# One GpSimd chain for two layer norms, a reordered start and looped expert programs in a Mamba and MoE block

## What is computed

```python
x = x + mamba(layernorm(x))      # in_proj 256 -> 2*512, causal conv of 4 taps, silu,
                                 # delta = softplus(dt_proj(...) + b), 16 states per channel:
                                 # h[t] = exp(delta*A)*h[t-1] + delta*B*xc ; y = h.C + D*xc
                                 # out_proj(y * silu(z))
x = x + moe(layernorm(x))        # shared: sq_relu(x @ Ws1) @ Ws2
                                 # routed: top 2 of 8 experts, prob = trunc(softmax weight)
```

## Time and profile before

| What | Value |
|---|---|
| Median of 3 runs | 1568.24 us |
| The profiled execution's own time | 1566.09 us |
| Its span, first to last instruction | 1564.0 us |
| Busy share PE / DVE / ACT / POOL | 93% / 94% / 80% / 90% |
| Chain that ended last, by engine | DVE 30%, ACT 19%, PE 18%, issue 16%, POOL 11% |
| DMA over the span | 106.49 MB, mean 68 GB/s |
| Granted TensorE clock | 0.999 |

### The profile page before, as it was taken

How to read it: one execution, slowest core, us unless ns; L and a number is a source line. 1 busy time by engine, 2 the same in 40 slices (tenths; PEclk the granted TensorE clock), 3 DMA queues, 4 the chain that set the end, 5 groups by cost and what they waited for, 6 DMA issues and landing times.

```text
span 1564.0 us, 39669 instructions
## 1 busy us (share of the span) xinstructions
PE 1452.4 (93%) x15308; PEld 1129.9 (72%) x15308; DVE 1474.4 (94%) x1773; ACT 1258.2 (80%) x2100; POOL 1410.5 (90%) x1248
## 2 busy tenths in 40 slices
PE   8789999999999999999999999999999999998987
PEld 4566777776776777777776777777777677777876
DVE  6999999999999999999999999999999999998886
ACT  7987887887888888887887888888887887788762
POOL 2899999999999999999999989999998999999994
PEclk9999999999999999999999999999999999999999
DMA  5103031040402204031040402304031040301301
GB/s 165 56 3 136 2 109 57 9 157 3 145 20 69 96 3 163 2 97 69 7 159 3 137 28 57 109 3 163 2 98 67 3 149 2 137 15 53 113 15 42
DMA packets 78514, 106.49 MB, mean 68 GB/s; under 512 B 42289, under 2 KB 67761, under 8 KB 70130
## 3 DMA queue, kind: packets, MB, share of 16 engines
q1 hardware_dynamic: 78322, 103.92, 20.5%
...
## 4 chain that ended last, share of the span: by engine, by line
DVE 30%; ACT 19%; PE 18%; issue 16%; POOL 11%; DMA 2%; SPq 2%; DVEq 1%; ACTq 0%; POOLq 0%
DVE hs L966 26%; POOL hs L1254 9%; PE BX L236 8%; ACT da L630 8%; PE Y L296 4%; SPq L1383 2%; DMA cb<-c_scratch 2%; PE Y L260 2%; ACT xc L697 1%; ACT xp L665 1%; PE PB L346 1%; ACT x2n L767 1%; ACT u L735 1%; DVE st L978 1%; DVE Y L997 1%
## 5 line engine op out<-in xcount | busy, mean ns | idle before, releaser
L1254 POOL TENSOR_TENSOR hs<-hs,cb 128x1024 f32<-128x1024 f32 x512 | 1211.3, 2367 | 65.6 <-DVE hs L966 43.6
L966 DVE TENSOR_TENSOR_SCAN hs<-da,BX 128x512 f32<-128x512 f32 x1024 | 1165.5, 1201 | 57.9 <-PE BX L236 48.4
L630 ACT ACTIVATE da<-delta,a_neg 128x511 f32<-128x511 f32 (+1 forms) x1024 | 663.5, 711 | 24.9 <-DVE hs L966 24.4
L260 PEld LDWEIGHTS Y<-ident,hs 128*128 128x128 f32 x4096 | 463.7, 141 | 96.5 <-issue 61.5
L260 PE MATMUL Y<-ident,hs 128*128 128x128 f32 x4096 | 511.5, 273 | 11.3 <-POOL hs L1254 11.2
L236 PE MATMUL BX<-bd,uT 32*128 32x128 f32 x8192 | 300.4, 283 | 85.3 <-DVE hs L966 80.3
L236 PEld LDWEIGHTS BX<-bd,uT 32*128 32x128 f32 x8192 | 251.6, 186 | 145.4 <-DVE hs L966 143.0
L296 PE MATMUL Y<-xnT,w_in 128*128 128x512 f32 x240 | 117.6, 612 | 0.9 <-ACT xnT L646 0.9
L665 ACT ACTIVATE xp<-Y 128x512 f32<-128x512 f32 x60 | 35.9, 598 | 99.4 <-PE Y L296 99.0
L321 PE MATMUL PA<-w_in,xnT 128*128 128x512 f32 x240 | 114.4, 599 | 0.0
L997 DVE SCALAR_TENSOR_TENSOR Y<-xp,w_conv,Y 128x512 f32<-128x512 f32 x120 | 88.8, 740 | 2.3 <-ACT Y L667 0.6
...
## 6 DMA issues: line engine op xcount, KB each, us to landing
...
c_scratch<-dbc SPq DMA_DIRECT2D x64, 8.0 KB, 1.5
```

Of the source, the lines that this page charges most:

```text
L260: mm = e.matmul(Y[(G * c + g) % 2][:, t * P:(t + 1) * P], hs[:, k % HR, q, t * P:(t + 1) * P], ident[:, :], is_transpose=True, start=False ...
L630: e.activation(da[:, k % DR, q, h:], delta[:, g, h:], ACT.Exp, scale=a_neg[:, g, n:n + 1]).then_inc(s_da, 1)
L966: e.tensor_tensor_scan(hs[:, k % HR, q, :], da[:, k % DR, q, :], BX[:, :].rearrange("p (t n) -> p n t", n=RT)[:, n % RT, :], float(c % HV) ...
L1254: e.tensor_tensor(hs[:, k % HR, :, :], hs[:, k % HR, :, :], cb[:, Q * p:Q * p + Q, :], ALU.mult).then_inc(s_hc, 1)
```

## The change

It has three parts.

1. In chunks 1 to 12 POOL computes `rstd` and `shift` of both norms in one chain over eight columns instead of two over four, at step 21; the statistics tiles of the two norms lie side by side for that. In chunk 0 the first norm's chain moves from step 25 to step 21. Chunks 13 to 15 keep the second norm's chain at step 21.
2. In the preparation of chunk 0, ACT's norm of chunk 1 stands behind the second silu; `dbc` is evacuated by DVE and the first `u` computed by DVE; the z tiles 1, 2 and 3 and the first skip product are made at other places; the first decay is split around the copy of `uT`. Eight matmuls of the identity into `PA` are added on PE in chunk 0 at step 3.
3. The routed programs of PE, ACT and DVE become loops over the chunks, with DVE shifting `prob` by one chunk in each pass.

The core of the diff, where `BOTH` is (1, 12); left out are the declarations, the counts of the semaphores that the joint chain shifts, the move of ACT's norm of chunk 1 out of its old place, the split of `act_exp`, POOL's wait in place of its first `u`, and the routed program of ScalarE:

```diff
@@ -457,17 +460,17 @@
             e.wait_ge(s_const, 7)
             pe_dbc(e, 0, 0)
             pe_dbc(e, 0, 1)
-            pe_z_first(e, 3, (0,))
             pe_dt(e, 0, 0)
             pe_bt(e, 0)
             pe_dt(e, 0, 1)
-            pe_z_first(e, 3, (1,))
-            pe_z_first(e, 2)
+            pe_z_first(e, 3)
             pe_ut(e, 0, 0)
+            pe_z_first(e, 2, (0,))
             e.wait_ge(s_d1_out, 1)
             pe_bx(e, 0)
             pe_trc(e, 1, 0)
             pe_trc(e, 1, 1)
+            pe_z_first(e, 2, (1,))
             for c in range(NQ):
                 for s in range(S):
                     k = S * c + s
@@ -483,6 +486,11 @@
                         pe_ut(e, c, 2)
                     if c == 0 and s in (0, 4, 8, 12):
                         pe_xp(e, G + s // 4)
+                    if c == 0 and s == 3:
+
+                        e.wait_ge(s_pa_out, a_use["trc", 1, 1] + 1)
+                        for _ in range(8):
+                            e.matmul(PA[:, 0:P], ident[:, :], ident[:, :], start=True, stop=True)
                     if c and on(c + 1) and s in (4, 12):
                         pe_xp(e, G * c + s // NP + 6)
                     if s == 28 and on(c + 1):
@@ -813,12 +820,12 @@
             act_xp_first(e, 2)
             act_xp_first(e, 3)
             act_silu_first(e, 1)
+            act_norm(e, 1)
             act_silu_first(e, 2)
             act_z_first(e, 0)
-            act_z_first(e, 1)
             act_silu_first(e, 3)
             e.preload_act_table_set(EXPS)
-            act_dbc(e, 0)
+            act_z_first(e, 1)
             e.wait_ge(s_wt, 16 * 9)
             e.activation(a_neg[:, :, :], a_log[:, :, :], ACT.Exp).then_inc(s_aneg, 1)
             e.wait_ge(s_aneg, 1)
@@ -826,14 +833,14 @@
             act_softplus(e, 0, 0)
             act_softplus(e, 0, 1)
             e.wait_ge(s_aneg, 2)
-            act_exp(e, 0)
+            act_exp(e, 0, (0,))
             act_ut(e, 0, 0)
+            act_exp(e, 0, (1,))
             act_z_first(e, 3)
-            act_z_first(e, 2)
             act_exp(e, 1)
             act_trc(e, 1, 0)
             act_trc(e, 1, 1)
-            act_skip(e, 0, 0)
+            act_z_first(e, 2)
             act_exp(e, 2)
             for c in range(NQ):
                 for s in range(S):
@@ -1123,10 +1132,18 @@
             dve_stats(e, 2, 0)
             dve_stats(e, 2, 1)
             dve_aggr(e, 2)
+            e.wait_ge(s_pa, a_use["dbc", 0, 0] + 1)
+            e.tensor_copy(dbc[0:FX, :].rearrange("f (j q t) -> f q j t", j=J, q=RT),
+                          PA[0:FX, :].rearrange("f (q j t) -> f q j t", j=J, q=RT)).then_inc(s_pa_out, 1)
             dve_stats(e, 3, 0)
             dve_stats(e, 3, 1)
             dve_bd(e, 0)
             dve_delta(e, 0, 0)
+            e.wait_ge(s_pb_out, b_use["dt", 0, 0] + 1)
+            e.wait_ge(s_xc, 1)
+            e.tensor_tensor(u[:, 0, :].rearrange("p (j q t) -> p q j t", j=J, q=RT),
+                            delta[:, 0, :].rearrange("p (q j t) -> p q j t", j=J, q=RT),
+                            xc[:, 0, :].rearrange("p (q j t) -> p q j t", j=J, q=RT), ALU.mult).then_inc(s_u, 1)
             dve_bd(e, 1)
             dve_delta(e, 0, 1)
             dve_bd(e, 2)
@@ -1276,24 +1293,30 @@
         def pool_rstd(e, c):
             e.wait_ge(s_mv, TB * (c + 1))
             e.wait_ge(s_xn, c)
-            e.tensor_tensor(ve[:, :], mv[:, :, 1], epsv[:, :], ALU.add).then_inc(s_ve, 1)
-            e.tensor_tensor(neg[:, :], mv[:, :, 0], minus[:, :], ALU.mult).then_inc(s_neg, 1)
+            n = TB
+            if BOTH[0] <= c - 3 <= BOTH[1]:
+                n = 2 * TB
+                e.wait_ge(s_mv2, TB * (c - 3))
+                e.wait_ge(s_xn2, c - 4)
+            e.tensor_tensor(ve_b[:, 0:n], mv_b[:, 0:n, 1], epsv[:, 0:n], ALU.add).then_inc(s_ve, 1)
+            e.tensor_tensor(neg_b[:, 0:n], mv_b[:, 0:n, 0], minus[:, 0:n], ALU.mult).then_inc(s_neg, 1)
             e.wait_ge(s_ve, c + 1)
-            e.tensor_tensor(rstd[:, :], ve[:, :], mhalf[:, :], ALU.pow).then_inc(s_rs, 1)
+            e.tensor_tensor(rstd_b[:, 0:n], ve_b[:, 0:n], mhalf[:, 0:n], ALU.pow).then_inc(s_rs, 1)
             e.wait_ge(s_neg, c + 1)
             e.wait_ge(s_rs, c + 1)
-            e.tensor_tensor(shift[:, :], neg[:, :], rstd[:, :], ALU.mult).then_inc(s_sh, 1)
+            e.tensor_tensor(shift_b[:, 0:n], neg_b[:, 0:n], rstd_b[:, 0:n], ALU.mult).then_inc(s_sh, 1)
 
         def pool_rstd2(e, c):
             e.wait_ge(s_mv2, TB * (c + 1))
             e.wait_ge(s_xn2, c)
-            e.tensor_tensor(ve2[:, :], mv2[:, :, 1], epsv[:, :], ALU.add).then_inc(s_ve2, 1)
-            e.tensor_tensor(neg2[:, :], mv2[:, :, 0], minus[:, :], ALU.mult).then_inc(s_neg2, 1)
-            e.wait_ge(s_ve2, c + 1)
-            e.tensor_tensor(rstd2[:, :], ve2[:, :], mhalf[:, :], ALU.pow).then_inc(s_rs2, 1)
-            e.wait_ge(s_neg2, c + 1)
-            e.wait_ge(s_rs2, c + 1)
-            e.tensor_tensor(shift2[:, :], neg2[:, :], rstd2[:, :], ALU.mult).then_inc(s_sh2, 1)
+            n = c + 1 - BOTH[1]
+            e.tensor_tensor(ve2, mv2[:, :, 1], epsv[:, 0:TB], ALU.add).then_inc(s_ve2, 1)
+            e.tensor_tensor(neg2, mv2[:, :, 0], minus[:, 0:TB], ALU.mult).then_inc(s_neg2, 1)
+            e.wait_ge(s_ve2, n)
+            e.tensor_tensor(rstd2, ve2, mhalf[:, 0:TB], ALU.pow).then_inc(s_rs2, 1)
+            e.wait_ge(s_neg2, n)
+            e.wait_ge(s_rs2, n)
+            e.tensor_tensor(shift2, neg2, rstd2, ALU.mult).then_inc(s_sh2, 1)
 
         def pool_gap(e, c):
             e.wait_ge(s_max, TB * (c + 1))
@@ -1334,11 +1357,11 @@
                             pool_u(e, c + 1, 0)
                         if s == 31:
                             pool_u(e, c + 1, 1)
-                    if s == 21 and on(c - 1):
+                    if s == 21 and c > BOTH[1]:
                         pool_rstd2(e, c - 1)
                     if s == 30 and on(c - 1):
                         pool_gap(e, c - 1)
-                    if s == 25 and on(c + 3):
+                    if s == 21 and on(c + 3):
                         pool_rstd(e, c + 3)
 
 
@@ -1485,43 +1509,55 @@
...
         def routed_tensor(e):
             e.wait_ge(r_w, 32)
-            for c in range(NQ):
-                e.wait_ge(r_x, 16 * (c + 1))
+            with e.Fori(0, NQ) as c:
+                e.wait_ge(r_x, 16 * c + 16)
                 for i in range(NE):
-                    m = NE * c + i
-                    e.wait_ge(r_re, m)
+                    if i:
+                        e.wait_ge(r_re, NE * c + i)
                     for kk in range(KD):
                         mm = e.matmul(PA[:, :], wr1[:, i, kk, :], xnT[0][:, kk, :], start=(kk == 0), stop=(kk == KD - 1))
                     mm.then_inc(r_h, 1)
-                    e.wait_ge(r_sq, m + 1)
-                    e.wait_ge(r_add, TB * m)
+                    e.wait_ge(r_sq, NE * c + i + 1)
+                    if i:
+                        e.wait_ge(r_add, TB * NE * c + TB * i)
                     for t in range(TB):
                         mm = e.matmul(Y[t // 2][:, (t % 2) * DM:(t % 2 + 1) * DM], hT[:, t * P:(t + 1) * P], wr2[:, i, :],
                                       start=True, stop=True)
                     mm.then_inc(r_y, 1)
 
...
         def routed_vector(e):
-            for c in range(NQ):
-                e.wait_ge(r_acc, 16 * (c + 1))
+            rest = da[:, :, :, :].rearrange("p k q t -> p (k q t)")[:, 0:(NQ - 1) * TB * NE].rearrange(
+                "p (c t n) -> p c t n", c=NQ - 1, t=TB)
+            with e.Fori(0, NQ) as c:
...
-                    m = NE * c + i
-                    e.wait_ge(r_y, m + 1)
-                    e.wait_ge(r_add, TB * m)
+                    e.wait_ge(r_y, NE * c + i + 1)
+                    if i:
+                        e.wait_ge(r_add, TB * NE * c + TB * i)
                     for t in range(TB):
                         e.scalar_tensor_tensor(
                             out=x1[:, t, :], in0=Y[t // 2][:, (t % 2) * DM:(t % 2 + 1) * DM],
-                            scalar=prob[:, c, t, i:i + 1], in1=x1[:, t, :], op0=ALU.mult,
+                            scalar=prob[:, 0, t, i:i + 1], in1=x1[:, t, :], op0=ALU.mult,
                             op1=ALU.add).then_inc(r_add, 1)
+
+                e.wait_ge(r_add, TB * NE * c + TB * NE)
+                e.tensor_copy(rest, prob[:, 1:NQ, :, :]).then_inc(r_mv, 1)
+                e.wait_ge(r_mv, 2 * c + 1)
+                e.tensor_copy(prob[:, 0:NQ - 1, :, :], rest).then_inc(r_mv, 1)
+                e.wait_ge(r_mv, 2 * c + 2)
...
```

More of the change, by code:

```diff
@@ L98, in mamba_moe @@
         mask = sb("mask", [P, KT])
-        mhalf = sb("mhalf", [P, TB])
-        minus = sb("minus", [P, TB])
-        epsv = sb("epsv", [P, TB])
+        mhalf = sb("mhalf", [P, 2 * TB])
+        minus = sb("minus", [P, 2 * TB])
+        epsv = sb("epsv", [P, 2 * TB])
         halo0 = sb("halo0", [P, G, K - 1])
```

(3 more changed lines are left out.)

57 lines of the change are left out of this document (30 added, 27 removed).

## The result

| | Before | After |
|---|---|---|
| Median (lowest to highest) | 1568.03 us, 4 runs (1567.34 to 1568.41) | 1560.89 us, 4 runs (1560.09 to 1561.75) |
| Own time of the profiled execution | 1566.09 us | 1560.9 us |
| Its span | 1564.0 us | 1559.1 us |

The changed kernel is faster by 0.45%: ratio 0.9955, 95% interval 0.9938 to 0.9972. The forecast was 1562.9 us in a range of 1560.8 to 1566.0, so the median lies inside by 0.1 us, at the lower end. Later comparisons ran the kernel before 27 times on another occasion, median 1566.97 us (1565.65 to 1568.56); against these the changed kernel, run again, stands at 0.9964 (0.9951 to 0.9978). The own time is longer than the span by 2.1 us before and by 1.8 after: 0.3 of the 5.2 us between the two profiled executions lie outside the span.

What follows compares the result with a forecast made beforehand. The prediction saw a DVE and PE cycle of 5.85 us as the untouched floor; gains of 2.1 + 0.4 + 2.8 = 5.3 us took the median from 1568.24 to 1562.9 us, own range 1562.0 to 1564.2, 8 in 10 range 1560.8 to 1566.0.

Steps and rivals of the forecast that it cites:

- The floor: DVE and PE alternating: four scans (4.55 us), then `pe_bx` (1.17); every 5.85 us, 256 times, 1498 us, untouched by the change.
- Part 1: POOL's joint norm chain: waits of steps 28 to 30 in even chunks go, a smaller one appears earlier; 2.1 us gained.
- the new wait: Steps 24 to 26 of six even chunks: the longer chain makes POOL late at step 23, costing 0.18 us each.
- Rivals 2 and 3: Joint chain only moves its wait, `pe_bx` 0.6 late (1565.0, chance 0.12); or new wait hidden, start gains 1.2 (1560.8, 0.12).
- Part 2: Preparation of chunk 0: first scan 1.16 us earlier, but `xp` waits for z tile 2's copy, leaving 0.4 us.
- Part 3: End of the span: PE's late branch over its routed program, for which SP waits 3.0 us, shortens; 2.8 us gained.
- Rival 1: End of the span: PE's branch stays slow despite the loops, giving 1565.7, no change; chance 0.15.
- Rival 4, the clock: Chunk 0, steps 0 to 8: PE's clock falls to 1.2 GHz, pairs take about 10 us for 5.85; chance 0.03.
- It decides from two such pairs on: Two pairs of steps at PE's lower clock, 2 x 4.2 us lost, would outweigh the 5.3 us gained.
- A PE clock below 1.00: Listed sign that the forecast is wrong: PE's granted clock under its full 2.4 GHz.
- with the same distance the median becomes 1562.9: Last step: profiled own time 1560.8 plus the 2.1 us by which before's profiled execution lay below its median of 1568.24.
- rival 3: Start keeps its gain (1.2 us) and the joint chain's added wait is hidden (3.4 us): 1560.8; chance 0.12.

## Why the prediction was right, and where it was not

- **The floor.** The cycle of 5.85 us stands as it did (some 45 of the 256 pairs take 5.90, in both kernels); everything that moved lies in single pairs, the preparation and the end.
- **Part 1**, forecast 2.1: measured 6 x 0.36 and 0.1 in chunk 0, 2.3. The power took 1638 ns for 1.63; the new wait in pairs 24 to 26 is 0.16 for 0.18. Two points of rows 5 were enough for a third, since cost per column stayed the same. Rivals 2 and 3 put the new wait at 0.6 and at nothing; neither was so.
- **Part 2**, forecast 0.4: measured 0.52. The wait for z tile 2 is there by name, and its removal gives 0.64 more. xp's matmuls began at 37.05 for 37.2. "The eight matmuls ... cost nothing" held, but I didn't see what they may give: 0.6 us in executions in which the clock falls there.
- **Part 3**, forecast 2.8: measured 2.8 by SP's wait, alone and together. Rival 1 fell; the doubt that "no row shows a PE branch that is fast" is answered by 0.49 us.
- **Rival 4, the clock**, was the badly described one. Its lower level did come, but in chunk 15 too, which I hadn't named, and it cost 0.5 to 0.9 us a time, not 4.2: the clock was low for a few microseconds, part of which DVE's scans cover. "It decides from two such pairs on" is thereby wrong: two events are 1.3 us (as in the run without the eight matmuls), not enough to turn the sign. "A PE clock below 1.00" was a badly chosen sign of being wrong: by the mean of the span it held for the kernel before as well (0.999), and by the stretch it came true in chunk 15 without the forecast failing by it.
- **The step that failed** is the last of the sum: "with the same distance the median becomes 1562.9". The forecast for the profiled execution's own time, 1560.8, met 1560.9, but partly by luck: the three parts gave 5.6 us for 5.3, chunk 15 took 0.8 back, and the own time's excess over the span fell by 0.3, which no term had. The 2.1 us between before's profiled execution and its median were no property of the kernel. The three first runs lay high: the median of 27 is 1566.97, 0.9 over the profiled one, and after's profiled execution lies on its median. Part of such a distance goes with the clock: the nine of the 27 executions with a mean granted clock of 0.999, which the profiled one has, average 1565.9 us, the two with 0.995 average 1568.4. Whether that holds for the three first runs isn't on record.
- **Luck in the number.** The measured 1560.9 lies outside the range that the forecast gave itself, 1562.0 to 1564.2, and on rival 3's 1560.8, though neither the hidden wait nor the full gain of the start that rival 3 stands on came about. The terms of the sum were right and the last subtraction was not. As a ratio the forecast is 0.9966, and the measured ones are 0.9955 and 0.9964.
